# Routed experts: all thirty-two row gathers issued ahead of the thirty-two result stores on GpSimd's queue

## What is computed

```python
scores = softmax(xf @ gate_w.T)                      # xf: 4096 x 128, E = 64
_, idx = top_k(scores + gate_b, K)                   # K = 6
weights = take_along_axis(scores, idx, axis=1)
flat_e = idx.reshape(-1)
order = argsort(flat_e)
se = flat_e[order]
counts = bincount(flat_e, length=E)
pos = arange(T * K) - (cumsum(counts) - counts)[se]
tok = order // K
xb = zeros((E, CAP, D)).at[se, pos].set(xf[tok], mode='drop')      # CAP = 64
h = silu(einsum('ecd,eid->eci', xb, w1)) * einsum('ecd,eid->eci', xb, w3)   # I = 88
yb = einsum('eci,edi->ecd', h, w2)
y = zeros_like(xf).at[tok].add(yb[se, min(pos, CAP - 1)] * wf[:, None])
```

## Time and profile before

| | us |
|---|---|
| median of 3 runs (lowest, highest) | 1488.04 (1482.0, 1488.44) |
| the profiled execution, device time | 1487.69 |
| its span, first to last instruction | 1485.7 |

### The profile page before, as it was taken

One profiled execution on the slowest core, in us unless ns is written; L12 is line 12 of the kernel. 1 busy time (PEld: TensorE's weight loads), 2 busy tenths in 40 slices (PEclk: granted clock), 3 DMA queues, 4 the chain that ended last, 5 costly groups with the idle time before them and its releaser, 6 DMA issues. The chain is left out here.

```text
span 1485.7 us, 28531 instructions
## 1 busy us (share of the span) xinstructions
PE 1256.5 (85%) x9347; PEld 716.3 (48%) x9347; DVE 1071.1 (72%) x2801; ACT 784.5 (53%) x1090; POOL 353.0 (24%) x343
## 2 busy tenths in 40 slices
PE   7599999999998999999999785069389679799993
PEld 4344444444433444444433553058246457687883
DVE  5299999999987999999970697733067665566565
ACT  4306877777765777777778362011044343235441
POOL 5320000000000000000000331475223144767652
PEclk9757999999977999999998897555599989999997
DMA  5661222211222012221100014386350000122244
GB/s 192 253 204 55 84 84 84 84 53 34 84 84 85 19 67 84 84 84 55 56 36 21 29 44 122 109 140 147 140 202 1 0 2 23 53 67 84 69 125 128
DMA packets 75549, 125.18 MB, mean 84 GB/s; under 512 B 11684, under 2 KB 46866, under 8 KB 75339
## 3 DMA queue, kind: packets, MB, share of 16 engines
q1 hardware_dynamic: 68299, 110.28, 21.9%
q0 software_dynamic: 7104, 13.02, 4.1%
HBM read 61.16 MB, written 66.29 MB: 86 GB/s over the span
## 5 line engine op out<-in xcount | busy, mean ns | idle before, releaser
L802 DVE TENSOR_REDUCE mx<-psum 128x1 f32<-128x512 f32 x1024 | 622.0, 681 | 64.2 <-PE psum L655 64.0
L754 ACT ACTIVATE probs<-psum 128x1024 f32<-128x1024 f32 x512 | 519.3, 1025 | 167.5 <-PE psum L672 160.6
L655 PE MATMUL psum<-akT,aqT 32*128 32x512 f32 x1024 | 391.8, 536 | 26.0 <-PEq L63 14.3
L691 PE MATMUL psum<-probs,vaug 128*32 128x256 f32 x4096 | 338.5, 409 | 2.3 <-issue 2.2
L672 PE MATMUL psum<-aqT,akT 32*128 32x512 f32 x1024 | 265.1, 513 | 8.3 <-DMA aqT<-mT 4.0
L655 PEld LDWEIGHTS psum<-akT,aqT 32*128 32x128 f32 x1024 | 184.3, 196 | 81.7 <-DVE mx L802 54.7
L672 PEld LDWEIGHTS psum<-aqT,akT 32*128 32x128 f32 x1024 | 98.9, 189 | 220.8 <-issue 189.6
L691 PEld LDWEIGHTS psum<-probs,vaug 128*32 128x32 f32 x4096 | 86.7, 111 | 132.0 <-ACT probs L754 69.8
L415 POOL TENSOR_TENSOR vaug<-vrows,bv_sb 128x256 f32<-128x256 f32 x16 | 11.5, 729 | 560.0 <-PE psum L691 560.0
L2071 POOL DMA_INDIRECT pair_rows<-yo,dest x78 | 77.5, 993 | 54.2 <-DVE dest L2570 40.5
L2062 POOL DMA_INDIRECT slot_rows<-slotrows,slot x64 | 62.1, 970 | 31.2 <-issue 14.8
(11 more groups left out here) (306 smaller groups left out, 1826.8 us busy)
## 6 DMA issues: line engine op xcount, KB each, us to landing
slot_rows<-pads SPq DMA_DIRECT2D x32, 585.0 KB
pick_rows<-zeros SPq DMA_DIRECT2D x48, 256.0 KB
yk<-pick_rows SPq DMA_DIRECT2D x8, 1536.0 KB, 7.3
aqT<-query_operands SPq DMA_DIRECT2D x16, 512.0 KB, 4.0
akT<-key_operands SPq DMA_DIRECT2D x16, 512.0 KB, 4.8
xg<-slot_rows SPq DMA_DIRECT2D x78, 65.0 KB
query_operands<-qhi SPq DMA_DIRECT2D x8, 512.0 KB
key_operands<-khi SPq DMA_DIRECT2D x8, 512.0 KB
```

The lines of the kernel that those rows point to most:

```text
L655: last = e.matmul(bank[:], qT[u % NG][r, i * P:(i + 1) * P], kT[u % NG][r, c * 512:(c + 1) * 512], start=True, stop=True)
L691: last = e.matmul(ctxp[h * R:(h + 1) * R, q], vaug[g][:, kt, h, :], probs[:, (2 * k + h // 2) % SLOTS, h % 2, q], start=(kt == 0 and part ...
L754: a.activation(probs[:, n % SLOTS, :, :], scores[:, n % 2, :, :], ACT.Exp)\
L802: dve.reduce_max(mx[:, h, i, c:c + 1], bank[:], X_AXIS).then_inc(tp_free, 1)
```

## The change

`AHEAD`, the number of buffers of gathered rows, goes from 5 to 8, and GpSimd issues the gathers of all eight groups before the first store. `xg` grows from 20 KB to 32 KB of each partition, and the stage has eight semaphores for gathered rows where it had five. The other engines' lists stay as they are, but for the numbers of the buffers and semaphores.

```diff
-        YB, AHEAD = 4, 5
+        YB, AHEAD = 4, NGR
...
-            for g in range(AHEAD):
+            for g in range(NGR):
                 gather(g)
             for g in range(NGR):
                 scatter(g)
-                if g + AHEAD < NGR:
-                    gather(g + AHEAD)
```

## The result

The changed kernel takes 1496.74 us (median of 20 runs, 1485.77 to 1516.18) where the kernel before, run beside it, takes 1488.58 (20 runs, 1475.38 to 1509.05). The ratio is 1.0068, with a 95% interval of 1.0036 to 1.0101: the change makes the kernel some 10 us slower (5 to 15). The forecast was +1.5 us.

A forecast was written before the change was run, and what follows sets the result against it. The prediction took PE to set the stage's pace, except 17 us bound by transfers with an 8.0 us stall. Its terms, 0 + 0 + 0 + 1.5 = +1.5 us on 1487.69, gave 1489.2 us, range 1484.0 to 1496.0.

The forecast's parts named there:

- What bounds the stage: Routed experts' stage: transfers bind 985.9 to 1002.8 us, then PE; one 8.0 us stall awaits group 3's weights.
- GpSimd's issues: GpSimd's queue: 32 gathers in a row end at 1000.7 instead of 1021.3 us, first stores later, cost 0.
- The late landing of the first stores: Group 0's stores free a buffer for group 4's results: landed by 1014.4, needed after 1024.9 us, cost 0.
- Group 3's weights: Stall before group 3's product: earlier gathers delay its weights by +1.5 us, between +0.5 and +3.3.
- the lower bound: Group 3's weights: both queues keep their full-load shares, SP's 46.1% and 0.155 MB/us, giving +0.5 us.
- Group 4's weights: Before group 4's product: four more gathers, up to 4.4 us, covered by 4.7 us of slack, cost 0.
- a sign of being wrong: PE's timeline: a second stall in front of group 4 or 5 would show the prediction wrong.
- The rival of one packet for one: DMA engines alternate packets between two queues, delaying group 3's weights by +4.1 us, 1491.8 us in all; chance 0.14.
- Starved weights: Group 3's weights get next to nothing until all twelve gathers are served: +11.7 us, 1499.4 us; chance 0.10.
- a shrinking stall: Group 3's stall shrinks as group 0's stores go: up to 8.0 us faster; chance 0.06 whole, 0.10 part.
- The range: Whole kernel: 1484.0 to 1496.0 us, with about 0.10 left out above and 0.10 below.
- Group 5's: Group 5's weights land at about 1019.5 us, PE needs them at 1021.5: covered by 2 us.

The follow-up runs named there:

- e3: The changed kernel with four buffers of expert weights instead of two; ratio 0.9919 to the kernel before.
- e2: The changed kernel with each empty slot gathering a row of its own instead of row 4095; ratio 0.9866 to the kernel before.
- e12: The kernel before, unchanged, profiled once more; 105.1 us from the first gather to the next stage's first product.
- e1: The kernel before with eight buffers and semaphores for gathered rows but GpSimd's old order; ratio 0.990 to the kernel before.
- e8: The changed kernel, unaltered, run once more; 114.4 us from the first gather to the next stage's first product.
- e9: The changed kernel with a row of its own for each empty slot, timed again in more rounds; ratio 0.9938 to the kernel before.

## Why the prediction was wrong

**What bounds the stage: right.** The stall in front of group 3 is a wait for weights held back by gathers; more weight buffers (e3) and cheaper gathers (e2) each take it away.

**GpSimd's issues: right.** Gathers without a gap in 40 us, stores of groups 0 and 1 late without harm, GpSimd ahead of PE again from group 2 on (0.90 us of idle there) and waiting 8.65 and 3.8 us later. The late landing of the first stores harmed nobody.

**Group 3's weights, +1.5 (0.5 to 3.3): right in size, in part by luck.** 8.3 us in the changed kernel's two profiles against 6.3 in the three of the old order, +2.0; a single execution varies by as much. But the lower bound, to which the figure was set near, let SP's queue keep its share of 46% and 0.155 MB/us; from 996 to 1002 it had 36.3% and 0.107 MB/us. That this share falls when gathers stand in GpSimd's queue without a break is what the next step needed. (The weights of a group are 1.08 MB in 344 packets, 256 of 2816 B and 88 of 4096 B, where the prediction has 1.056 MB in 375; it changes little.)

**Group 4's weights, "covered, with nothing to spare": this step failed.** It was +0 in the sum and measured 4.9 and 7.3, mean 6.1; 2.0 + 6.1 is the stage's 7.5 within the variation. It is also the second stall that the prediction named as a sign of being wrong. The sum set four more gathers, 4.4 us, against 4.7 us of slack. The landing took 21.9 us instead of 13.7, 8.2 more. From the first gather to that landing the queues did this, first before the change (960.7 to 1008.2), then changed (965.3 to 1021.6):

```profile
q0 software_dynamic: 1565, 3.72, 65.0%
q1 hardware_dynamic: 1062, 2.88, 19.2%
...
q0 software_dynamic: 1840, 4.32, 64.0%
q1 hardware_dynamic: 1298, 3.58, 22.1%
```

In time of all engines that is 30.9 + 9.1 us before and 36.0 + 12.4 after: 5.1 us more for GpSimd's queue, near the 4.4, and 3.3 more for SP's. So the price of a gather, 1.1 us, was right, and yet the weights were held up by nearly twice the 4.4 charged. SP's 3.3 us are 0.70 MB of weights that were asked for only from 1015 us on (group 4's for the second product and group 5's for the first) and moved while PE still waited for group 4's first ones.

The trace's semaphore increments, 16 for each transfer, show how that goes. The 32 of group 4's two halves are spread from 1009.5 to 1021.6 us, and nine of group 5's come ahead of the last. A transfer has landed when its last part has, and a sum over all 16 engines knows nothing of this spread. But the spread isn't all of it: the mean of the 32 moved as well, from 43.7 us behind the first gather to 50.7 (from 42.5 in the three profiles of the old order to 50.7 in both of the new), again more than the 4.4 charged and more than the slack. Here are the queues in 13 us of each kernel, from 34.5 us behind the first gather, when SP is asking for these weights; first before the change (995.2 to 1008.2), then changed (999.8 to 1012.8):

```profile
q0 software_dynamic: 594, 1.09, 58.0%
q1 hardware_dynamic: 598, 1.59, 38.4%
...
q0 software_dynamic: 389, 1.06, 70.0%
q1 hardware_dynamic: 370, 1.05, 28.0%
```

GpSimd's queue moved nearly the same bytes, SP's a third less. In the same 13 us SP's queue moved 1.29 MB in e12 and 1.42 in e1, where the weights were in earlier, and 1.02 in e8. In the old order stores stood between the gathers, 205 packets more in all; after the change there were only gathers. That the smaller share comes from this is argued from these rows; no run has it by itself. So the step failed in that it charged the weights with the added gathers' own time and nothing else, neither for the smaller share beside an unbroken row of gathers nor for the last part of a transfer. How the 8.2 us divide between the two no run here shows.

**The rival of one packet for one** asked for +4.1 us and is nearer than the forecast. From 980 to 984 the count was 247 of SP's to 92 of GpSimd's; in the changed kernel, from 1002 to 1008, it is 121 to 189. Without the packets of 4 B that is 220 to 67 and then 106 to 126. So the ratio isn't fixed: with gathers queued the whole time the weights fall to somewhat fewer packets than the gathers. The Trainium skill's page "DMA: Bandwidth & Descriptors", section "Queues, rings and completion order", has each engine take packets in turn from the queues with work. By that rule the second stretch is near what it says, and the first is not, perhaps because not every engine had gathers queued; no view here shows single engines. The rival too put its cost at group 3 and not at group 4.

**Starved weights** (+11.7) and **a shrinking stall** (-8.0) didn't come. **The range** ended at +8.3 and the median came at +9: too narrow on the upper side, since group 4's cover, with 0.3 us to spare by the prediction's own figures, got no chance of failing. Group 5's held: its weights landed at 1025.7, 4.5 us before the product at 1030.25.

**What wasn't asked at all** was why a gather costs 1.1 us of the engines when the same bytes as weights cost 0.4. The rows had it: 98.7% for 0.61 MB in the earlier trace rows is 0.10 MB/us, where 51.3% for 1.01 MB in the earlier trace rows is 0.33 MB per us of full engines. That factor of three was the real finding of this profile.

## What to carry to other kernels

Issuing transfers early isn't free where other transfers with a deadline share the DMA engines: for each deadline, compare what is queued ahead with the slack, and keep a reserve of the same size again: here 4.4 us of added gathers held the weights up by 8.2. Where padding reads a dummy row, let each slot read another row: here one added VectorE instruction takes more than half off each gather, and makes the order of issue matter little. A prefetch moved ahead is also moved ahead of other loads in its own queue; ask who waits for those (7.0 us in e3).

## What the runs showed of the hardware

- Gathers of 128 rows of 1 KB took 0.97 us of the 16 DMA engines when most rows are the same one, and 0.44 us when they differ, be it over 4096 rows or over the same 128 each time.
- The last part of a 352 KB transfer landed up to 22.5 us after its issue under such gathers (e8; 21.9 in the changed kernel's first profile), against 4.5 to 5.1 us with none queued.
- Beside an unbroken row of such gathers SP's queue moved 1.02 and 1.05 MB in 13 us, beside gathers and stores in turn 1.29 to 1.59 MB.
- 135 runs of eleven programs, the kernel before among them, follow the mean granted clock of TensorE by 9.9 us per 0.01, with 1.9 us left over. Stretches outside this stage differ by up to 14 us between executions of one program (915.2 and 929.1 us up to the search for slots in e2 and e9); to judge 10 us in 1490, stage lengths from profiles told more than medians.
